# A four-layer cross-attention stack on one core: small layers' tails merged into single stages, one layer's keys computed in the tail before, and its first query group stored alone

## The chip, the core and the metric

The kernel runs on one core of a Trainium2 chip. It is one program, launched once, in 32-bit floats. The metric is the device time of one execution in microseconds (us). The core has five engines with an instruction stream each: TensorE (PE in the rows; PEld is its weight load), VectorE (DVE), ScalarE (ACT), GpSimd (POOL) and SyncE (SP), which here only issues transfers.

## What is computed

Four layers follow one another on 1024 tokens (4 batches of 256) with 256 features; the context has the same size. Layer 0 is a large attention block with 16 heads of 128 and is not touched. Layers 1 and 3 are alike (16 heads of 16, keys from the context and from the tokens), layer 2 has 32 query heads of 8 over 8 key heads. Cut to what matters:

```python
def layer_1_and_3(x, latents):                    # latents: the tokens, x: the context
    h = concatenate([x, latents], axis=1)
    q = latents @ q_w + q_b
    kmat, v = split(h @ kv_w + kv_b)
    attn_out = softmax(mask(q kmat / 16)) v
    attn_out = attn_out @ out_w + out_b + latents
    out = attn_out * rsqrt(mean(attn_out**2) + 1e-6) * postnorm_w
    return gelu(out @ mlp_w1 + mlp_b1) @ mlp_w2 + mlp_b2 + latents

def layer_2(hidden, context):
    q, k, v = hidden @ Wq + bq, context @ Wk + bk, context @ Wv + bv
    x = softmax(q k / sqrt(8) + mask) v @ Wo + bo + hidden
    return (x - mean) * rsqrt(var + 1e-6) * gamma + beta
```

The keys of layer 2 come from the context alone, so they don't depend on layer 1.

## The kernel before

The program is a row of stages. Each is a block in which every engine runs its own list of instructions, ordered by hand and tied by semaphores; at the end of a block all engines meet, so the next block starts when the last of them, SyncE with its waits on transfers included, is through. Activations lie in SBUF as 8 tiles of 128 tokens by 256 features (`core.x`, in the rows `x_tok`), and transposed as 2 chunks of 128 features (`kt`) by 1024 tokens, worked in halves of 512. Products that feed a softmax or an MLP are made from a high and a low part of each operand (`hi` is a rounded copy, `lo` the rest), which costs a copy on ScalarE and a subtraction on VectorE or GpSimd per tile.

Layers 1 and 3 run the stages `pair_projections` (p), `pair_attention` (s), `project_out` (o), `rms_turn` (r) and `mlp` (m). Layer 2 runs `turn` (t, it transposes the tokens), `wide_projections` (p), `wide_attention` (s), `project_out` (o) and `final_norm` (n). The prefix of a tile's name in the rows is the stage's letter.

- `project_out`: SyncE loads the output weight and the bias row; TensorE transposes the attention's output `o_all` (16 transposes into `t_ps`), VectorE copies the four chunks to `oT`, adds the bias row to the residual tile by tile, and then adds each product `y_ps` to it.
- `rms_turn`: SyncE loads the first MLP weight (`w1_raw`), ScalarE rounds it, GpSimd subtracts (`w1_lo`). VectorE takes the statistics of 8 tiles, GpSimd the power -0.5 of each half, ScalarE scales tiles 0 to 3, VectorE tiles 4 to 7, TensorE transposes, ScalarE and VectorE write the two parts of the MLP's input, `h_hi` and `h_lo`.
- `wide_projections`: TensorE makes keys (two groups of 512 tokens), then queries (four groups), then values. Each group goes VectorE (bias) to ScalarE (high) to VectorE (low) to SyncE, which stores it in HBM (`k_stack`, `q_stack`) and loads it again in the layout of the attention (`k_st`, `q_st`; `load_keys` and `load_queries` are four transfers each). The block ends when both query chunks are stored and the first half of batch 0's queries has come back.
- `wide_attention` goes over 32 quads of heads, eight for each batch; SyncE loads the queries and keys of the later ones beside it.
- `final_norm` takes the statistics, normalises, scales and shifts 8 tiles in a row on VectorE.

## Time and profile before

| | us |
|---|---|
| median of 3 executions | 1364.05 (1360.95 to 1368.05) |
| the profiled execution | 1362.59 |
| its span in the profile | 1360.8 |
| layer 1: last attention output to the MLP's first matmul | 873.53 to 899.38 |
| layer 2: last tile of layer 1 to the attention's first matmul | 947.69 to 979.64 |
| layer 2: last attention output to layer 3's first transpose | 1105.16 to 1132.71 |
| layer 3: last attention output to the MLP's first matmul | 1286.67 to 1312.69 |

The profile is of one execution. A row of the timeline gives the start, the time from start to end in us, engine, line, operation, tiles, and a count; in brackets how long the engine had stood idle and what released it (PEq and POOLq are the sequencers of those engines, and a line of `with nc.Block()` there is the meeting at a block's end). Instructions of one engine overlap a little, so a row of eight is shorter than eight single ones. An fp32 matmul stands as two records.

### The profile page before, as it was taken

How to read it: one execution, taken by the hardware profiler on the slowest of the kernel's cores; microseconds unless marked ns; L12 is line 12 of the kernel's file. 1: busy time of each engine (PE TensorE's matmuls, PEld its weight loads, DVE VectorE, ACT ScalarE, POOL GpSimd, SP SyncE). 2: the span in 40 equal slices, each digit the busy share in tenths (PEclk: the TensorE clock that was granted, in tenths of full speed). 3: DMA queues.
4: the chain of work that ended last, by engine and by line, in shares of the span. 5: the costliest groups of instructions: out<-in, count | busy, mean ns of one | idle time of the engine just before them, and what ended most of it. 6: DMA issues, size and time to landing. Idle time of an engine off the chain costs nothing. (4 is left out here: it accounts for less than half of the span.)

```text
span 1360.8 us, 27452 instructions
## 1 busy us (share of the span) xinstructions
PE 1222.3 (90%) x9144; PEld 1008.0 (74%) x9144; DVE 984.0 (72%) x2228; ACT 724.9 (53%) x1644; POOL 491.9 (36%) x638
## 2 busy tenths in 40 slices
PE   5999999999799999998699699869599977699969
PEld 5999999998699999997598355558377756455558
DVE  5778888778788788887564588474488865689464
ACT  5666566566666567666532277341166632177441
POOL 4744554453654454442240000030199940000030
PEclk9999999999899999999799599879799997699889
DMA  5111001100311110100305873020760013874020
GB/s 177 47 32 33 22 17 31 31 24 0 106 32 32 32 31 23 31 15 0 98 1 107 106 83 40 13 79 2 210 124 2 2 52 74 126 80 57 13 66 32
DMA packets 55406, 70.90 MB, mean 52 GB/s; under 512 B 6696, under 2 KB 47404, under 8 KB 52976
## 3 DMA queue, kind: packets, MB, share of 16 engines
q1 hardware_dynamic: 53704, 65.83, 23.3%
q10 hardware_dynamic: 1600, 3.76, 1.0%
q8 instruction: 57, 0.93, 0.3%
q14 instruction: 45, 0.37, 0.1%
HBM read 46.79 MB, written 8.13 MB: 40 GB/s over the span
## 5 line engine op out<-in xcount | busy, mean ns | idle before, releaser
L993 ACT ACTIVATE a_prob<-a_s_ps,a_negmax 128x257 f32<-128x257 f32 x256 | 119.0, 476 | 93.6 <-DVE a_negmax L1075 93.6
L2085 DVE TENSOR_REDUCE s_mx<-s_s_ps 128x2 f32<-128x1024 f32 x128 | 151.9, 1211 | 18.3 <-PE s_s_ps L2130 18.0
L2070 ACT ACTIVATE s_probT<-s_st_ps 128x512 f32<-128x512 f32 x256 | 132.2, 606 | 56.3 <-PE s_st_ps L2144 54.0
L934 POOL TENSOR_TENSOR x_v_hi<-a_v_sum,x_one 128x512 fp32r<-128x512 f32 x60 | 63.2, 1053 | 244.5 <-DVE a_v_sum L1064 244.4
L1874 POOL TENSOR_SCALAR s_below<-s_masked,s_mx 128x256 f32<-128x256 f32 x256 | 117.8, 480 | 28.8 <-DVE s_mx L1902 28.0
L605 POOL TENSOR_TENSOR rstd<-base,power 128x4 f32<-128x4 f32 x4 | 4.0, 1009 | 334.4 <-DVE base L622 334.4
L1090 DVE TENSOR_TENSOR a_pT_lo<-a_t_ps,a_pT_hi 128x512 fp32r<-128x512 f32 x128 | 88.2, 689 | 37.3 <-ACT a_pT_hi L1006 35.6
L1075 DVE TENSOR_REDUCE a_negmax<-a_s_ps 128x2 f32<-128x514 f32 x128 | 87.0, 688 | 23.8 <-PE a_s_ps L1136 23.7
L1902 DVE CUSTOM_DVE_ANT_0 s_masked<-s_s_ps,l_mask 128x256 f32<-128x256 f32 x256 | 90.7, 421 | 15.7 <-PE s_s_ps L1939 15.7
L1006 ACT ACTIVATE a_pT_hi<-a_t_ps 128x512 fp32r<-128x512 f32 x128 | 76.6, 599 | 46.8 <-PE a_t_ps L1190 43.2
L1134 PE MATMUL a_s_ps<-x_k_hi,x_q_hi 128*128 128x258 f32 x256 | 74.7, 292 | 11.2 <-ACT a_prob L993 5.4
L1887 ACT ACTIVATE s_probT<-s_st_ps 128x512 f32<-128x512 f32 x128 | 69.7, 595 | 28.2 <-PE s_st_ps L1949 28.1
L1134 PE MATMUL a_o_ps<-a_pT_hi,x_v_hi 128*128 128x256 f32 x256 | 81.1, 317 | 0.0
L2130 PE MATMUL s_s_ps<-l_k_st,l_q_st 49*128 49x512 f32 x192 | 67.5, 544 | 15.0 <-PEq L1583 8.6
L1009 ACT ACTIVATE a_oT_hi<-a_o_ps,a_hc 128x256 fp32r<-128x256 f32 x128 | 60.7, 474 | 37.0 <-PE a_o_ps L1136 29.7
L1190 PE MATMUL a_t_ps<-ident,a_prob 128*128 128x128 f32 x512 | 77.2, 273 | 3.3 <-ACT a_prob L1001 2.0
L936 POOL TENSOR_TENSOR x_v_lo<-a_v_sum,x_v_hi 128x512 fp32r<-128x512 f32 x60 | 77.4, 1290 | 4.7
L2144 PE MATMUL s_st_ps<-l_q_st,l_k_st 50*128 50x256 f32 x384 | 69.9, 337 | 10.0 <-DMA l_q_st<-s_mxT 9.8
L1136 PE MATMUL a_s_ps<-x_k_hi,x_q_lo 128*128 128x258 f32 x256 | 72.8, 285 | 0.0
L2144 PEld LDWEIGHTS s_st_ps<-l_q_st,l_k_st 50*128 50x128 f32 x384 | 47.9, 203 | 33.6 <-DMA l_q_st<-s_mxT 11.9
L1135 PE MATMUL a_s_ps<-x_k_lo,x_q_hi 128*128 128x258 f32 x256 | 72.7, 284 | 0.0
L1136 PE MATMUL a_g_ps<-a_wo_hi,a_oT_lo 128*128 128x256 f32 x256 | 72.6, 283 | 0.0
(293 smaller groups left out, 4047.2 us busy)
## 6 DMA issues: line engine op xcount, KB each, us to landing
a_wo_raw<-L_xattn_wo SPq DMA_DIRECT2D x16, 256.0 KB, 3.4
x_wqk_raw<-L_xattn_wq SPq DMA_DIRECT2D x31, 128.0 KB, 2.3
x_wqk_raw<-L_xattn_wk SPq DMA_DIRECT2D x31, 128.0 KB, 2.3
x_wv_raw<-L_xattn_wv SPq DMA_DIRECT2D x15, 256.0 KB, 3.2
l_k_st<-k_second SPq DMA_DIRECT2D x12, 256.0 KB, 9.3
l_k_st<-k_stack SPq DMA_DIRECT2D x16, 192.0 KB
l_q_st<-q_stack SPq DMA_DIRECT2D x12, 192.0 KB
x_vbias<-L_xattn_bias_v SPq DMA_DIRECT2D x2, 1024.0 KB, 7.1
```

The lines of the kernel that those rows point to most:

```text
L936: nc.gpsimd.tensor_tensor(lo, raw, hi.bitcast(F32), ALU.subtract).then_inc(z.v_split, 1)
L993: nc.scalar.activation(prob[:, n % 2, qt, 0:NK], s_ps[:, n % 2, qt, 0:NK], ACT.Exp, bias=negmax[:, n % 2, qt:qt + 1], accum_out=den[:, n % ...
L1075: nc.vector.tensor_reduce(negmax[:, n % 2], s_ps[:, n % 2, :, 0:NK], AX.X, ALU.max, negate=True).then_inc(z.max_done, 1)
L1090: nc.vector.tensor_tensor(pT_lo[:, n % 2], t_ps[:], pT_hi[:, n % 2].bitcast(F32), ALU.subtract).then_inc(z.t_out, 1)
L1134: nc.tensor.matmul(out, a_hi, b_hi, start=start, stop=False)
L1136: return nc.tensor.matmul(out, a_lo, b_hi, start=False, stop=stop)
L1190: mm = nc.tensor.transpose(t_ps[:, at:at + P], prob[:, n % 2, qt, kt * P:(kt + 1) * P], core.ident[:])
L1874: nc.gpsimd.tensor_scalar(below[:, i % 2, h, qt], masked[:, i % 2, h, qt], -1.0, mx[:, i % 2, h, qt:qt + 1], ALU.mult, ALU.add).then_inc(z ...
L1902: nc.vector.tensor_tensor_reduce(out=masked[:, i % 2, h, qt], in0=s_ps[:, h, qt], in1=mask[:, i // NQ * QT + qt], scale=1.0, scalar=-3.0e3 ...
L2070: nc.scalar.activation(probT[:, third % 2, n // 4, n // 2 % 2, n % 2], st_ps[:, u % 3], ACT.Exp, scale=c.scale).then_inc(z.exp_done, 1)
L2085: nc.vector.tensor_reduce(mx[:, i % 2, qt, a::2], s_ps[:, n % 2], AX.X, ALU.max).then_inc(z.max_done, 1)
L2144: mm = nc.tensor.matmul(st_ps[:, u % 3, j * S:(j + 1) * S], k[:, a, kt * P:(kt + 1) * P], q[:, a], start=True, stop=True)
```

## The change

Nothing is computed otherwise; the numbers are the same operations in other places.

- The stages `project_out` and `rms_turn` of layers 1 and 3 become one block, `project_and_rms`; `project_out` and `final_norm` of layer 2 become `project_and_scale`. In them VectorE and ScalarE copy two chunks each, VectorE takes a tile's statistics right behind its addition, and all scaling by the norm is ScalarE's (eight tiles instead of four).
- The output weight and bias row are loaded during the attention (`OutWeights`), and the bias is added to the residual there, by GpSimd: in layers 1 and 3 in `pair_attention`, into the memory of the late heads' high keys (`k_high`), in layer 2 in `wide_projections`, into `core.x`.
- The projection weights of layers 2 and 3 are loaded at the end of the attention before.
- The keys of layer 2 are made and stored in layer 1's tail (`WideKeys`); layer 1's `mlp` lets ScalarE wait for their three stores before its first instruction.
- `turn` is part of `wide_projections`, whose query groups now go by token half first. Only group 0 is stored there, by three transfers of 256 KB, and only batch 0's mask is loaded; groups 1 to 3 and the other masks are SyncE's in the attention.
- The MLP's `hid` buffer lies in `o_all`.

```diff
+    def keys(self, pe, half):
+        KW, core = self.front.KW, self.core
+        for kt in range(KT):
+            mm = self.nc.tensor.matmul(self.ps(half), core.wkv[:, kt, 0:KW], core.cT[:, kt, self.cols(half)],
+                                       start=(kt == 0), stop=(kt == KT - 1))
+        mm.then_inc(self.k_done, 1)
+
+    def high(self, act, half):
+        cols = self.cols(half)
+        act.wait_ge(self.k_done, half + 1)
+        self.nc.scalar.activation(self.f[:, cols], self.ps(half), ACT.Identity, bias=self.bias).then_inc(self.f_done, 1)
+        act.wait_ge(self.f_done, half + 1)
+        self.nc.scalar.activation(self.hi[:, cols], self.f[:, cols], ACT.Copy).then_inc(self.hi_done, 1)
+
+    def low(self, pool, half):
+        cols = self.cols(half)
+        pool.wait_ge(self.hi_done, half + 1)
+        self.nc.gpsimd.tensor_tensor(self.lo[:, cols], self.f[:, cols], self.hi[:, cols].bitcast(F32), ALU.subtract
+                                     ).then_inc(self.lo_done, 1)
+
+    def store(self, sp):
+
+        for part, (kept, slots) in enumerate(((self.hi, (0, 2)), (self.lo, (1,)))):
+            sp.wait_ge((self.hi_done, self.lo_done)[part], 2)
+            for n in slots:
+                sp.dma_start(self.front.k_stack[:, n], kept[:].bitcast(F32)).then_inc(self.front.k_stored, 16)
...
+                if wide:
+                    act.wait_ge(wide.k_stored, 3 * 16)
...
-            rms_turn(core, f"r{layer}", src, w, EPS, scale)
+            c, o_all, weights, dst = front
+            project_and_rms(core, f"r{layer}", c, o_all, weights, dst, w, EPS, scale, wide)
...
-                sp.dma_start(mask[:], ins["mask_Bx1xSxS2_ff0"].rearrange("b o (t p) k -> p (b o t) k", p=P)
-                             ).then_inc(mask_in, 16)
-
-                def stores(g):
-                    is_k, m, _ = groups[g]
-                    for part in range(2):
-                        sp.wait_ge((qk_hi, qk_lo)[part], g + 1)
-                        store(sp, part, is_k, m)
-
-                stores(1)
-                stores(3)
-                sp.wait_ge(k_stored, 16 * 3)
-                load_keys(c, sp, k_stack, k_st, 0, first_in)
-                stores(5)
-                sp.wait_ge(q_stored[0], 16 * 3)
-                load_queries(c, sp, q_stack, q_st, 0, slice(0, c.NQ // 2), first_in)
-                sp.wait_ge(mask_in, 16)
-                sp.wait_ge(q_stored[1], 16 * 3)
-                sp.wait_ge(first_in, 16 * 8)
+                pool.wait_ge(z.tile_turned, 2 * KT)
+                weights.add_row(pool, core.x, z.row_in)
...
+                sp.wait_ge(front.k_stored, 3 * 16)
+                load_keys(c, sp, front.k_stack, k_st, 0, z.first_in)
+                load_mask(core, sp, mask, 0, z.mask_in)
+                weights.load_row(sp, z.row_in)
+                for part in range(2):
+                    sp.wait_ge((z.q_hi, z.q_lo)[part], 1)
+                    q_late.store(front, sp, 0, (high(0), low(0)), part, z.q_stored)
+                sp.wait_ge(z.q_stored, 3 * 16)
+                load_queries(c, sp, front.q_stack, q_st, 0, slice(0, c.NQ // 2), z.first_in)
+                sp.wait_ge(z.mask_in, 16)
+                sp.wait_ge(z.first_in, 16 * 8)
...
+                    dve.wait_ge(z.q_done, g + 1)
+                    nc.vector.tensor_scalar(whole(g), q_ps[:, g], bq[:, m:m + 1], c.scale, ALU.add, ALU.mult
+                                            ).then_inc(z.q_f, 1)
+                    dve.wait_ge(z.q_hi, g + 1)
+                    nc.vector.tensor_tensor(low(g), whole(g), high(g).bitcast(F32), ALU.subtract).then_inc(z.q_lo, 1)
...
-                load_queries(c, sp, q_stack, q_st, 0, slice(NQ // 2, NQ), batch_in[0])
-                for b in range(1, B):
-                    load_keys(c, sp, k_stack, k_st, b, batch_in[b])
-                    load_queries(c, sp, q_stack, q_st, b, slice(0, NQ), batch_in[b])
+                def store(g):
+                    for part in range(2):
+                        q_late.store(front, sp, g, (q_late.hi[:, g - 1], q_late.lo[:, g - 1]), part, q_stored[g - 1])
+
+                store(1)
+                load_mask(core, sp, mask, 1, batch_in[1])
+                sp.wait_ge(q_stored[0], 3 * 16)
+                load_queries(c, sp, front.q_stack, q_st, 0, slice(NQ // 2, NQ), batch_in[0])
+                load_keys(c, sp, front.k_stack, k_st, 1, batch_in[1])
+                load_queries(c, sp, front.q_stack, q_st, 1, slice(0, NQ), batch_in[1])
+                for g in (2, 3):
+                    store(g)
+                for b in range(2, B):
+                    load_mask(core, sp, mask, b, batch_in[b])
+                    load_keys(c, sp, front.k_stack, k_st, b, batch_in[b])
+                for g in (2, 3):
+                    sp.wait_ge(q_stored[g - 1], 3 * 16)
+                for b in range(2, B):
+                    load_queries(c, sp, front.q_stack, q_st, b, slice(0, NQ), batch_in[b])
+                weights.load(sp, z.out_in)
+                sp.wait_ge(z.out_in, 16 + core.load_projections(sp, 3, z.out_in))
...
+                pool.wait_ge(unit_in[1], c.UNIT + 4 * 16)
+                pool.wait_ge(unit_in[2], c.UNIT)
+                weights.add_row(pool, a_tok, z.row_loaded)
...
+                    if first == 11:
+                        weights.load_row(sp, z.row_loaded)
+                        weights.load(sp, z.out_in)
+                sp.wait_ge(z.out_in, 16 + (core.load_projections(sp, 2, z.out_in) if L == 1 else 0))
...
+    def add_row(self, pool, dst, row_in):
+
+        pool.wait_ge(row_in, 16)
+        for t in range(TT):
+            self.core.nc.gpsimd.tensor_tensor(dst[:, t], self.core.x[:, t], self.row[:], ALU.add)
...
+    def copy_vector(self, dve, half):
+        out, ps = self.place(0, half)
+        dve.wait_ge(self.z.turned, KT * half + 1)
+        self.nc.vector.tensor_copy(out, ps).then_inc(self.z.copied_dve, 1)
+
+    def copy_scalar(self, act, half):
+        out, ps = self.place(1, half)
+        act.wait_ge(self.z.turned, KT * half + 2)
+        self.nc.scalar.activation(out, ps, ACT.Copy).then_inc(self.z.copied_act, 1)
+
+    def product(self, pe, t):
+        if t % 4 == 0:
+            pe.wait_ge(self.z.copied_dve, t // 4 + 1)
+            pe.wait_ge(self.z.copied_act, t // 4 + 1)
+        wait(pe, self.z.y_out, t - 3)
+        for kt in range(KT):
+            mm = self.nc.tensor.matmul(self.y_ps[:, t % 4, 0:D], self.oT[:, kt, t * P:(t + 1) * P],
+                                       self.weights.w[:, kt], start=(kt == 0), stop=(kt == KT - 1))
+        mm.then_inc(self.z.y_done, 1)
+
+    def add(self, dve, t):
+        dve.wait_ge(self.z.y_done, t + 1)
+        self.nc.vector.tensor_tensor(self.dst[:, t], self.y_ps[:, t % 4, 0:D], self.dst[:, t], ALU.add
+                                     ).then_inc(self.z.y_out, 1)
+
+    def observe(self, dve, t):
+        dve.wait_ge(self.z.y_out, t + 1)
+        observe(self.core, dve, self.dst, t, self.z)
...
+                low(0)
+                deviation(core, pool, 0, z, 0)
+                low(1)
+                deviation(core, pool, 1, z, 1)
+                if keys:
+                    for half in range(2):
+                        keys.low(pool, half)
...
+                out.turn(pe)
+                for t in range(TT):
+                    out.product(pe, t)
+                for half in range(2):
+                    if keys:
+                        pe.wait_ge(z.y_out, half + 5)
+                        keys.keys(pe, half)
+                    pe.wait_ge(z.normed_act, HT * (half + 1))
+                    for kt in range(KT):
+                        for i in range(HT):
+                            mm = nc.tensor.transpose(turned[:, KT * half + kt, i * P:(i + 1) * P],
+                                                     normed[:, HT * half + i, kt * P:(kt + 1) * P], core.ident[:])
+                        mm.then_inc(z.tile_turned, 1)
...
+                    out.copy_scalar(act, half)
+                ahead.prepare_scalar(act, z)
+                for t in range(4):
+                    normalise(t)
+                if keys:
+                    keys.high(act, 0)
+                for n in range(2):
+                    high(n)
+                for t in range(4, TT):
+                    normalise(t)
+                if keys:
+                    keys.high(act, 1)
+                for n in range(2, 4):
+                    high(n)
...
```

What VectorE does in layer 1's tail, where `o` and `r` name the stages, `a_o_all` and `a_k_high` the sum of residual and projection. Before:

```order
L2241 COPY o_oT<-o_t_ps 128x512 x4
L2245 TENSOR_TENSOR a_o_all<-x_tok,o_b_row 128x256 x8
L2249 TENSOR_TENSOR a_o_all<-o_y_ps,a_o_all 128x256 x8
L2197 UNCONDITIONAL_BRANCH
L609 UNCONDITIONAL_BRANCH
L614 BN_STATS stats<-a_o_all 128x6 x4
L617 BN_AGGR mv<-stats 128x2 x4
L620 TENSOR_TENSOR r_msq<-mv 128x4
```

Now (the first half; the second is alike, without the copies):

```order
L2212 COPY r_oT<-r_t_ps 128x512 x2
L2231 TENSOR_TENSOR a_k_high<-r_y_ps,a_k_high 128x256
L164 BN_STATS stats<-a_k_high 128x6
L2231 TENSOR_TENSOR a_k_high<-r_y_ps,a_k_high 128x256
L164 BN_STATS stats<-a_k_high 128x6
L2231 TENSOR_TENSOR a_k_high<-r_y_ps,a_k_high 128x256
L164 BN_STATS stats<-a_k_high 128x6
L2231 TENSOR_TENSOR a_k_high<-r_y_ps,a_k_high 128x256
L164 BN_STATS stats<-a_k_high 128x6
L2242 BN_AGGR mv<-stats 128x2 x4
L2332 TENSOR_TENSOR r_msq<-mv 128x4
L2334 SCALAR_TENSOR_TENSOR base<-r_msq,mv 128x4
```

The eight additions of the bias are gone, two of the four copies too, and every second row is a statistic where all of them stood behind the last addition.

ScalarE in the same tail, `w_w_hi` being the rounded first MLP weight and `r_k_f`, `r_k_hi` layer 2's keys. Before:

```order
L2204 UNCONDITIONAL_BRANCH
L588 UNCONDITIONAL_BRANCH
L1352 ACTIVATE w_w_hi<-w_w_raw 128x1024 x2
L593 ACTIVATE r_normed<-a_o_all,rstd 128x256 x4
L597 ACTIVATE w_h_hi<-r_turned,cols 128x512 x4
L583 UNCONDITIONAL_BRANCH
```

Now:

```order
L2298 UNCONDITIONAL_BRANCH
L2217 ACTIVATE r_oT<-r_t_ps 128x512 x2
L1299 ACTIVATE w_w_hi<-w_w_raw 128x1024 x2
L2308 ACTIVATE r_normed<-a_k_high,rstd 128x256 x4
L574 ACTIVATE r_k_f<-r_y_ps,cols 64x512
L576 ACTIVATE r_k_hi<-r_k_f 64x512
L2303 ACTIVATE w_h_hi<-r_t_ps,cols 128x512 x2
L2308 ACTIVATE r_normed<-a_k_high,rstd 128x256 x4
L574 ACTIVATE r_k_f<-r_y_ps,cols 64x512
L576 ACTIVATE r_k_hi<-r_k_f 64x512
L2303 ACTIVATE w_h_hi<-r_t_ps,cols 128x512 x2
L2259 UNCONDITIONAL_BRANCH
```

The two copies, four more scalings and the four instructions on the keys have come in, the scalings in two groups of four, each ahead of the two chunks of `w_h_hi` that need it.

SyncE in layer 2's projections. Before:

```order
L1751 DMA l_mask<-mask_Bx1xSxS_ff 128x8x256
L1735 DMA k_stack<-p_k_hi 8x8x1024 x2
L1735 DMA k_stack<-p_k_lo 8x8x1024
L1739 DMA q_stack<-p_q_hi 16x8x1024 x2
L1739 DMA q_stack<-p_q_lo 16x8x1024
L1692 DMA l_k_st<-k_stack 24x8x256 x4
L1739 DMA q_stack<-p_q_hi 16x8x1024 x2
L1739 DMA q_stack<-p_q_lo 16x8x1024
L1699 DMA l_q_st<-q_stack 24x4x256 x4
L1741 UNCONDITIONAL_BRANCH
```

Now:

```order
L1644 DMA l_k_st<-k_stack 24x8x256 x4
L1650 DMA l_mask<-mask_Bx1xSxS_ff 128x2x256
L2175 DMA a_b_out<-L_xattn_bo 128x256
L1672 DMA q_stack<-p_q_hi 16x8x512 x2
L1672 DMA q_stack<-p_q_lo 16x8x512
L1656 DMA l_q_st<-q_stack 24x4x256 x4
L1703 UNCONDITIONAL_BRANCH
```

The stores of the keys have gone into layer 1's tail, and one query store of half the size stands ahead of the four loads, where two full ones stood.

## Rows read from the trace of the kernel before

**Rows 1.** Busy time by engine (with counts), TensorE's granted clock, DMA share and GB/s.

```profile
885.00:899.30 14.30, 3.93 (x16) 3.13 (x16) 12.07 (x28) 6.46 (x10) 6.70 (x4) 0.61 0.22 73
```

**Rows 2.** Timeline of VectorE from the end of layer 1's attention to its MLP.

```profile
873.24 0.29 DVE L2096 TENSOR_TENSOR a_o_all<-s_ox_ps,s_rden 128x128 f32<-128x128 f32 x1
874.51 2.48 DVE L2241 COPY o_oT<-o_t_ps 128x512 f32<-128x512 f32 x4 [0.99 <-PE o_t_ps L2222]
...
885.02 1.41 DVE L614 BATCH_NORM_STATS2 stats<-a_o_all 128x6 f32<-128x256 f32 x4 [0.32 <-PEq L2197]
...
890.22 5.32 DVE L626 TENSOR_SCALAR r_normed<-a_o_all,rstd 128x256 f32<-128x256 f32 x4 [1.12 <-POOL rstd L605]
...
897.47 1.60 DVE L630 SCALAR_TENSOR_TENSOR w_h_lo<-r_turned,cols,w_h_hi 128x512 fp32r<-128x512 f32 x2 [0.61 <-ACT w_h_hi L597]
```

**Rows 3.** Timelines of SyncE's queue, ScalarE, GpSimd and TensorE in the same stretch.

```profile
884.97 0.89 SPq L1347 DMA_DIRECT2D w_w_raw<-L_xattn_mlp_w  x2
...
888.71 1.06 ACT L1352 ACTIVATE w_w_hi<-w_w_raw 128x1024 fp32r<-128x1024 f32 x1 [16.24 <-DMA w_w_raw<-L_xattn_mlp_w]
...
890.15 4.71 POOL L1357 TENSOR_TENSOR w_w_lo<-w_w_raw,w_w_hi 128x1024 fp32r<-128x1024 f32 x2
...
880.55 3.69 PE L2232 MATMUL o_y_ps<-o_w,o_oT 128*128 128x256 f32 x16 [0.15 <-DVE a_o_all L2249]
892.75 1.97 PE L640 MATMUL r_turned<-ident,r_normed 128*128 128x128 f32 x8 [8.50 <-ACT r_normed L593]
...
899.38 0.76 PE L1411 MATMUL m_h_ps<-w_h_hi,w_w_hi 128*128 128x512 f32 x1 [1.81 <-PEq L583]
```

**Rows 4.** Timeline of TensorE at the start of layer 3's MLP.

```profile
1312.69 0.47 PE L1411 MATMUL m_h_ps<-w_h_hi,w_w_hi 128*128 128x512 f32 x1 [1.81 <-PEq L583]
```

**Rows 5.** Timelines of VectorE, ScalarE, TensorE and SyncE's queue in layer 2's projections.

```profile
947.27 0.42 DVE L1474 TENSOR_TENSOR x_tok<-m_y_ps,x_tok 128x256 f32<-128x256 f32 x1 [2.45 <-PE m_y_ps L1413]
...
960.48 0.75 DVE L1799 TENSOR_SCALAR p_q_f<-p_qk_ps,cols 128x512 f32<-128x512 f32 x1 [0.37 <-PE p_qk_ps L1779]
961.14 0.68 DVE L1803 TENSOR_TENSOR p_q_lo<-p_q_f,p_q_hi 128x512 fp32r<-128x512 f32 x1
...
961.26 0.63 ACT L1822 ACTIVATE p_q_hi<-p_q_f 128x512 fp32r<-128x512 f32 x1 [1.09 <-DVE p_q_f L1799]
...
955.02 7.13 PE L1779 MATMUL p_qk_ps<-x_xT,wq 128*128 128x512 f32 x16
...
979.64 0.81 PE L1939 MATMUL s_s_ps<-l_k_st,l_q_st 24*128 24x256 f32 x8 [13.12 <-PEq L1741]
...
960.20 1.80 SPq L1739 DMA_DIRECT2D q_stack<-p_q_hi  x2
...
968.69 2.03 SPq L1739 DMA_DIRECT2D q_stack<-p_q_lo  x1
970.77 10.37 SPq L1699 DMA_DIRECT2D l_q_st<-q_stack  x8
```

**Rows 6.** Transfers of line 1739, the stores of `q_stack`: six of 512 KB.

```profile
DMA to landing us min/median/max: 4.9/6.9/8.9
```

**Rows 7.** Timelines of VectorE, GpSimd and TensorE in layer 2's tail.

```profile
1104.93 0.23 DVE L1914 TENSOR_TENSOR a_o_all<-s_ox_ps,s_rden 128x64 f32<-128x64 f32 x1
...
1114.02 0.43 DVE L2249 TENSOR_TENSOR x_tok<-o_y_ps,x_tok 128x256 f32<-128x256 f32 x1 [0.67 <-PE o_y_ps L2232]
...
1129.65 2.76 DVE L2296 TENSOR_TENSOR x_tok<-x_tok,n_b_row 128x256 f32<-128x256 f32 x8
...
1114.85 2.55 POOL L100 TENSOR_TENSOR parts_w_parts<-wkv,parts_w_parts 128x512 fp32r<-128x512 f32 x2
...
1109.44 8.86 PE L2232 MATMUL o_y_ps<-o_w,o_oT 128*128 128x256 f32 x32 [2.03 <-DMA o_w<-L_xattn_Wo]
...
1132.71 3.65 PE L1625 MATMUL p_turned<-ident,x_tok 128*128 128x128 f32 x16 [14.41 <-PEq L2262]
```

**Rows 8.** Timeline of VectorE in layer 1's MLP, while GpSimd subtracts there.

```profile
909.64 1.78 DVE L1457 TENSOR_TENSOR m_hid_lo<-m_hid,m_hid_hi 128x512 fp32r<-128x512 f32 x1
```

536 lines of the change are left out of this document (265 added, 271 removed).

## The prediction

> **What bounds the kernel now.** I first read the busy table by engine: TensorE is busy 90% of the span, so what can be won quickly lies where it stands. The 40 slices put these places between layers, and the timelines of the engines show four of them. In layer 1's tail the attention's last output ends at 873.53 [rows 2] and the MLP's first matmul starts at 899.38 [rows 3]: 25.85 us. In them VectorE works nearly without a gap, first on copies and sums, then on statistics [rows 2], and TensorE waits 8.5 us for the scaled tiles [rows 3]. The chain there is transposes, copies, products, sums, statistics, power, scaling, transposes, `h_hi`, `h_lo`, with a meeting of all engines in the middle, and the MLP weight is asked for only behind that meeting, at 884.97 [rows 3]. Layer 3's tail is the same, 1286.67 to 1312.69, 26.02 us [rows 4]. Layer 2's tail, 1105.16 to 1132.71, is 27.55 us, and TensorE stands 14.41 us in it, while VectorE passes over all tiles one pass after the other [rows 7]. The fourth place is layer 2's start, 947.69 to 979.64, 31.95 us: VectorE and ScalarE are through long before, and TensorE waits 13.12 us for the block's end [rows 5], which is SyncE's wait for stores of 512 KB that take 4.9 to 8.9 us to land [rows 6]. The last of them was issued at 970.72, and 8 us behind that is the block's end.
>
> **The change, part by part.** Times are counted from the end of the last attention output (0).
>
> Layer 1's tail. Transposes run 0.3 to 2.3 as now. The first copy starts about 1.0 in [rows 2] and takes some 0.7; with ScalarE taking every second one, none holds back the products, which before began at 3.1 and waited for the output weight and for VectorE. A weight that is loaded in the attention costs SyncE's queue one issue there and no one waits for it. Four tiles of product take 3.69 [rows 3], with the overlap some 0.87 each, so eight end at 9.3. VectorE adds (0.42, [rows 7]) and takes the statistic (1.41 for four, 0.41 singly, [rows 2]) in about 0.81 per tile: it keeps up with TensorE in the first half. The moments and the two small operations cost 0.8 per half, so the second half ends at 10.75 and its `base` at 11.55. The power takes 1.0 on GpSimd. The weight is asked for at 0.3; from issue to ScalarE's start it was 3.74 [rows 3], so ScalarE rounds it from 4.1 to 6.4 (1.06 each and a gap), GpSimd subtracts the first half from 5.2 to 7.6 (4.71 for two, [rows 3]), makes the first power until 8.65, subtracts again until 11.1, and makes the second power by 12.6. ScalarE scales four tiles by 10.4 (0.42 each). TensorE has meanwhile made the keys' first half: the queries' four groups take 7.13, so one group 1.8 [rows 5]: 9.3 to 11.1. Then come one after the other on ScalarE: two key operations (0.7 and 0.63) until 12.5, two `h_hi` until 13.8, four scalings until 15.45, two key operations until 16.8, two `h_hi` until 18.05. VectorE's last `h_lo` ends at 18.85, the last key store is issued at about 19.0, and with 0.3 for the meeting the MLP starts at **19.3**: 6.5 less. The four key instructions cost 2.6 of ScalarE's time here; without them it would be 17 to 18. The MLP's new wait for the key stores stands before ScalarE's table load. By the shortest landing of the larger stores, 4.9 [rows 6], the last one lands at 24, some 4.7 into the MLP, and by half that (half the bytes) at 21.5. Behind that wait stand the table load and the first activations, and TensorE can go on for four groups of 1.4 to 1.7 before it misses them. I take 0 for it, 3 at the other end.
>
> Layer 3's tail has no keys in it: the same chain gives 17.8 with all at full speed. The weight landed a microsecond later there, and its transposes may run at half clock, so I take **18.5**: 7.5 less.
>
> Layer 2's tail. Product and sums as above, 10.8. GpSimd now has to subtract the next layer's three weights (2.55 for two, [rows 7]) before it can make the first power: ScalarE rounds them from 3.1 on, GpSimd is through at 7.6, and the power, asked for at 7.3, is there at 8.6, when VectorE has just done tile 5. That costs nothing. ScalarE scales the tiles; VectorE is left with 16 operations of 0.345 (2.76 for eight, [rows 7]), in pairs with a wait of its own result between, 1.45 per two tiles: 11.4 to 17.45. The end is at **17.75**: 9.8 less. GpSimd's subtractions in this stretch left VectorE's addition at 0.43 [rows 7].
>
> Layer 2's start, counted from 947.69. The meeting between `turn` and the projections goes (3.4 us with the first copies), and the keys with their 3.6 on TensorE. Transposes end at 2.3, query group 0 at 4.1, its bias, high and low parts (0.75, 0.63, 0.68, [rows 5]) at 6.4. SyncE has issued the key loads, mask and row by 5.0; two stores took it 1.80 [rows 5], half rows less, so the last store is issued at about 7.5. These three are 256 KB each instead of six of 512 KB. From both sides: at the shortest landing, 4.9 [rows 6], they are in HBM at 12.4; with half of that at 10. I take 11.5. Four loads at some 0.6 are issued by 14, and landing takes 3.4 (the 3.74 of the MLP weight, [rows 3], less ScalarE's start): **17.4**, 14.5 less. Between 15.5 and 21. VectorE's work is no later than that: four groups in series at 2.3 are through at 13.3, the values at 15.7.
>
> Beside them run GpSimd's eight new additions, from about 8 on, 5 us by the 2.55 for two of twice the size [rows 7]. A VectorE subtraction of SBUF operands beside a GpSimd one in the MLP took 1.78 [rows 8] where it takes 0.68 alone [rows 5]. Three of the `q_lo` can be hit: up to 3.3 more, VectorE through at 19.0 instead of 15.7. The Trainium skill, SBUF — State Buffer, in the summary of its contention rules, says that a VectorE instruction with two SBUF inputs and a GpSimd instruction that reads SBUF exclude one another for their whole length. By that rule the block would end at up to 19.0 and not at 17.4, the sum 1.6 worse; the row agrees with the rule. I keep 17.4, since only what exceeds the transfers counts, and 19.0 goes into the range.
>
> The clock. TensorE's granted clock is 0.61 of full speed over layer 1's tail [rows 1]: it stood, and it starts the MLP at half speed (1.2 GHz), 0.76 for its first matmul [rows 3], while layer 3's MLP starts at full speed, 0.47 [rows 4], because 16 transposes ran just before it in one piece. Layer 1's MLP took 48.3, layer 3's 45.5 from first matmul to last sum: 2.8 for the clock. In the new tails the transposes stand in two pieces of 1 us with gaps of 2 to 4 us about them, so I expect layer 3's MLP to begin slowly too: **+2.8**; layer 1's has the keys in between, I take no change there.
>
> In the pair attentions GpSimd is idle, and its eight additions and SyncE's two loads cost nothing: VectorE's work there reads PSUM. The second half of batch 0's queries must be there four quads after the start of `wide_attention`, 14 us; SyncE stores, waits and loads them by 12 (2 for the stores, 4 to land, 2.4 and 3.4 for the loads). The price of a delay is small: 0 to 4.
>
> Sum: 6.5 + 7.5 + 9.8 + 14.5 - 2.8 = 35.5. The profiled execution took 1362.59 for a span of 1360.8, so 1327.1 for it; its time lies 1.46 below the median of 1364.05, so the median goes to **1328.5**.
>
> **The rivals.** (a) The waits take half the room: landing at the long end (+3.5 at layer 2's start), the second query half late (+4), the MLP's wait for the key stores (+3): about +10, 1338. For it speaks that store landings vary between 4.9 and 8.9 [rows 6]; against it that less is in flight. (b) The clock stays up through both tails: neither MLP starts slowly, 2.8 + 2.8 better, and ScalarE's order fits better than I think: 1321. (c) The change doesn't shorten the blocks: each tail is held by a chain I think covered, in layers 1 and 3 GpSimd with weight and power in one list, at layer 2's start the stores. Then only the copies' 1.4 and a meeting of 0.6 are won in each tail: 1358. Against it: GpSimd's list is 7.8 long and starts at 5. (d) Slower: `wide_attention` is starved. Its loads for batches 2 and 3 stand in SyncE's queue behind six more stores and a wait for them. From the point at which a round of stores and loads takes longer than the 30 us of eight quads, every batch adds the rest. It would have to take 42 us each time, three times 12, to eat 36 of gain: 1366 and more. A round is reckoned at 20.
>
> **How the numbers follow.** The forecast has a chance of 0.62, (a) 0.2, (b) 0.13, (c) 0.03, (d) 0.02. The range reaches from 1319 (b, with the short landings) to 1341 (a, with the contention's 1.6 and slow transposes). A measurement of this kernel can tell about 0.5% (7 us) from no change. The chance of slower is that of (d), that of no difference most of (c).
>
> **What would show it.** In the profile after: the MLPs start 19 and 18.5 us behind the last attention output, layer 3's transposes 17.8 behind layer 2's; the attention of layer 2 starts 17.4 us behind the last sum of layer 1, with TensorE waiting some 2 us at that meeting; `q_lo` rows of over 1 us show the contention; a wait of TensorE for `l_q_st` in quad 4 shows (a); the first matmul of an MLP at 0.47 or 0.76 shows the clock. I would be wrong above all if a store of 256 KB lands no faster than one of 512 KB.

## The result, and the profile after

| | before | changed |
|---|---|---|
| median of the runs, us | 1363.16 (1360.95 to 1368.05) | 1325.91 (1323.9 to 1328.42) |
| ratio to before | 1 | 0.9723, 95% interval 0.9691 to 0.9755 |
| profiled execution; its span | 1362.59; 1360.8 | 1325.39; 1323.2 |
| mean granted clock | 0.939 | 0.950 |

The change takes 37.3 us off the median (forecast 1328.5). The stages can be measured between rows that both kernels have: the end of the last attention output (`a_o_all`), the first matmul into `m_h_ps`, the end of the MLP's last sum (`x_tok<-m_y_ps`), the first `s_s_ps` matmul, and the first `p_turned` transpose. "Layer 3 up to the tail" holds its projections and its attention.

| stage, us | before | changed | gain |
|---|---|---|---|
| up to the end of layer 1's attention | 873.53 | 873.48 | 0.1 |
| layer 1's tail | 25.85 | 19.98 | 5.9 |
| MLP 1 | 48.31 | 47.71 | 0.6 |
| layer 2's start | 31.95 | 16.21 | 15.7 |
| layer 2's attention | 125.52 | 126.26 | -0.7 |
| layer 2's tail | 27.55 | 16.74 | 10.8 |
| layer 3 up to the tail | 153.96 | 155.02 | -1.1 |
| layer 3's tail | 26.02 | 18.15 | 7.9 |
| MLP 3 | 45.54 | 47.14 | -1.6 |

The gains add up to 37.6, the difference of the spans is 37.6. The three tails and layer 2's start give 40.3; the other stages together take 2.7 more than before.

Layer 1's tail, from the timelines of VectorE, TensorE, ScalarE and SyncE's queue of the changed kernel (start, length, engine and line, operation, count, in brackets the wait before it and what ended it). It answers [rows 2, 3]:

```profile
873.19 0.29 DVE L2074 TENSOR_TENSOR a_o_all<-s_ox_ps,s_rden 128x128 f32<-128x128 f32 x1
875.64 7.14 PE L2225 MATMUL r_y_ps<-a_w_out,r_oT 128*128 128x256 f32 x32
882.50 1.71 ACT L2308 ACTIVATE r_normed<-a_k_high,rstd 128x256 f32<-128x256 f32 x4 [2.46 <-POOL rstd L181]
885.04 0.16 DVE L2334 SCALAR_TENSOR_TENSOR base<-r_msq,mv 128x4 f32<-128x4 f32 x1
...
889.92 1.24 ACT L2303 ACTIVATE w_h_hi<-r_t_ps,cols 128x512 fp32r<-128x512 f32 x2
891.39 1.28 SPq L589 DMA_DIRECT2D k_stack<-r_k_lo  x1
893.46 0.76 PE L1358 MATMUL m_h_ps<-w_h_hi,w_w_hi 128*128 128x512 f32 x1 [3.53 <-PEq L2259]
```

The products start 2.2 behind the last output (3.1 before), the eight run through in 7.14, ScalarE scales the first four tiles while VectorE still sums the last four, and the chain ends with the last `h_hi` at 891.16 and the last key store at 892.67.

Layer 2's start, from the timelines of all engines; it answers [rows 5]:

```profile
940.75 0.42 DVE L1423 TENSOR_TENSOR x_tok<-m_y_ps,x_tok 128x256 f32<-128x256 f32 x1 [2.45 <-PE m_y_ps L1360]
947.95 0.60 SPq L1672 DMA_DIRECT2D q_stack<-p_q_lo  x1
950.58 6.40 POOL L2182 TENSOR_TENSOR x_tok<-x_tok,a_b_out 128x256 f32<-128x256 f32 x8 [6.05 <-DMA a_b_out<-L_xattn_bo]
950.82 1.04 DVE L1759 TENSOR_TENSOR l_q_lo<-p_q_f,l_q_hi 128x512 fp32r<-128x512 f32 x1 [0.70 <-ACT l_q_hi L1776]
952.33 1.57 SPq L1656 DMA_DIRECT2D l_q_st<-q_stack  x4
953.21 1.14 DVE L1759 TENSOR_TENSOR l_q_lo<-p_q_f,l_q_hi 128x512 fp32r<-128x512 f32 x1 [0.70 <-ACT l_q_hi L1776]
956.83 0.22 DVE L1764 TENSOR_TENSOR l_v_st<-p_v_ps,bv_row 128x64 f32<-128x64 f32 x1 [0.48 <-PE p_v_ps L1745]
957.38 0.81 PE L1910 MATMUL s_s_ps<-l_k_st,l_q_st 24*128 24x256 f32 x8 [0.58 <-PEq L1703]
```

SyncE issues the last of the three stores 7.4 us behind the last sum, has them 3.8 later and issues the loads. Before, TensorE waited 13.12 at this meeting [rows 5]; now 0.58. Three things end here close together: the last of the query and key loads lands at 956.49 (the trace's semaphore events), GpSimd's additions end at 956.98, VectorE's last value tile at 957.05. So in this execution it is VectorE that ends last, 0.33 before the first scores.

The ends of the two other tails, from the timelines of VectorE, TensorE and SyncE's queue; they answer [rows 4, 7]:

```profile
1094.55 0.76 DVE L2416 TENSOR_TENSOR x_tok<-x_tok,o_g_row 128x256 f32<-128x256 f32 x2
...
1099.33 0.75 DVE L2419 TENSOR_TENSOR x_tok<-x_tok,o_b_row 128x256 f32<-128x256 f32 x2
1100.38 3.65 PE L1577 MATMUL p_turned<-ident,x_tok 128*128 128x128 f32 x16 [7.43 <-PEq L2366]
...
1269.94 1.80 PE L2294 MATMUL r_t_ps<-ident,r_normed 128*128 128x128 f32 x8 [2.73 <-ACT r_normed L2308]
1273.55 0.77 PE L1358 MATMUL m_h_ps<-w_h_hi,w_w_hi 128*128 128x512 f32 x1 [1.81 <-PEq L2259]
```

The clock shows in the last three: sixteen transposes take 3.65, as they did before [rows 7], where the same sixteen take 1.94 at layer 2's start; eight take 1.80 here and 1.09 in the tail's first half; and MLP 3 starts with 0.77 where it had 0.47 [rows 4]. The granted clock over the end of that tail, from the view by stretches (length, busy time of PE, PEld, DVE, ACT, POOL, granted clock, DMA share, GB/s):

```profile
1265.00:1268.00 3.00, 1.09 (x8) 0.86 (x8) 2.38 (x11) 2.25 (x5) 2.53 (x2) 1.00 0.00 0
1268.00:1271.00 3.00, 1.06 (x6) 1.06 (x7) 0.94 (x2) 1.86 (x6) 0.14 (x1) 0.86 0.00 0
1271.00:1274.00 3.00, 1.19 (x5) 0.81 (x4) 1.50 (x2) 1.78 (x3) 0.00 (x0) 0.50 0.00 0
```

### The profile page after: what moved, and what is told of

Same layout as the page of the kernel before. It is cut to its first block and busy times, and to the rows that moved or that the text cites. A ratio compares the mean times of both kernels' runs of the same rounds, so it can differ in the third digit from the quotient of the medians.

```text
span 1323.2 us, 27397 instructions
## 1 busy us (share of the span) xinstructions
PE 1218.8 (92%) x9144; PEld 1005.9 (76%) x9144; DVE 961.0 (73%) x2179; ACT 737.7 (56%) x1670; POOL 511.6 (39%) x664
## 5 line engine op out<-in xcount | busy, mean ns | idle before, releaser
L2063 DVE TENSOR_REDUCE s_mx<-s_s_ps 128x2 f32<-128x1024 f32 x128 | 151.9, 1211 | 18.0 <-PE s_s_ps L2108 17.7
L1037 DVE TENSOR_TENSOR a_pT_lo<-a_t_ps,a_pT_hi 128x512 fp32r<-128x512 f32 x128 | 88.2, 689 | 37.3 <-ACT a_pT_hi L953 35.6
L2182 POOL TENSOR_TENSOR a_k_high<-x_tok,a_b_out 128x256 f32<-128x256 f32 x16 | 11.1, 733 | 223.7 <-DMA a_b_out<-L_xattn_out_b 223.7
L2122 PEld LDWEIGHTS s_st_ps<-l_q_st,l_k_st 50*128 50x128 f32 x384 | 48.4, 204 | 33.6 <-DMA l_q_st<-s_mxT 12.0
L1081 PE MATMUL a_g_ps<-a_wo_hi,a_oT_hi 128*128 128x256 f32 x256 | 72.5, 283 | 0.0
```

What stands on the lines that cost most here:

```text
L1037: nc.vector.tensor_tensor(pT_lo[:, n % 2], t_ps[:], pT_hi[:, n % 2].bitcast(F32), ALU.subtract).then_inc(z.t_out, 1)
L1081: nc.tensor.matmul(out, a_hi, b_hi, start=start, stop=False)
L2063: nc.vector.tensor_reduce(mx[:, i % 2, qt, a::2], s_ps[:, n % 2], AX.X, ALU.max).then_inc(z.max_done, 1)
L2122: mm = nc.tensor.matmul(st_ps[:, u % 3, j * S:(j + 1) * S], k[:, a, kt * P:(kt + 1) * P], q[:, a], start=True, stop=True)
```

## The experiments

Each is an edit of the changed kernel. The stages of all of them, in us between the rows named above, are of the execution that was profiled; the median is that of all executions, with that of the kernel before, run beside it. The edits were run in three groups on different chips, so medians of different groups are compared by their ratio to before:

| kernel | tail 1 | MLP 1 | start 2 | tail 2 | layer 3 | tail 3 | MLP 3 | median (of before beside it) |
|---|---|---|---|---|---|---|---|---|
| changed_again | 19.98 | 47.67 | 16.47 | 16.75 | 154.98 | 18.33 | 47.05 | 1326.44 (1364.68) |
| all_groups | 19.98 | 48.28 | 26.14 | 16.73 | 151.40 | 17.57 | 47.69 | 1331.56 (1362.02) |
| keys_back | 18.16 | 47.03 | 24.24 | 16.75 | 152.91 | 18.34 | 46.84 | 1331.18 (1362.02) |
| keys_back_no_row | 18.33 | 46.91 | 24.06 | 16.75 | 154.09 | 18.35 | 47.04 | 1328.40 (1364.68) |
| no_row | 19.98 | 47.76 | 16.12 | 16.73 | 154.76 | 18.67 | 48.37 | 1323.81 (1365.31) |
| residual_back | 26.32 | 48.08 | 15.22 | 22.66 | 155.19 | 23.43 | 47.76 | 1338.12 (1362.02) |
| adds_back | 20.55 | 47.70 | 15.90 | 21.58 | 151.18 | 19.86 | 48.30 | 1329.91 (1365.31) |
| sums_first | 23.96 | 47.35 | 16.48 | 19.59 | 151.27 | 22.76 | 46.91 | 1338.11 (1362.02) |
| keys_kept | 20.07 | 47.79 | 16.72 | 16.73 | 154.61 | 18.27 | 46.91 | 1324.90 (1365.31) |
| filled | 20.64 | 47.57 | 16.83 | 17.61 | 153.89 | 17.77 | 45.53 | 1323.81 (1365.31) |
| late_stores | 18.85 | 48.27 | 17.28 | 16.74 | 154.86 | 18.27 | 47.05 | 1324.52 (1364.68) |
| best | 18.86 | 45.53 | 16.49 | 16.74 | 151.22 | 17.76 | 45.50 | 1316.93 (1364.68) |

A stage that an edit doesn't touch repeats within 0.1 in tails 1 and 2, some 0.6 in layer 2's start, 1.1 in tail 3, 0.9 in MLP 1 and 1.5 in MLP 3. Layer 3's part scatters by 4. Most of the scatter of the MLPs and of layer 3 goes with the time at half clock, as is shown further on.

**The changed kernel again**, as the measure for keys_back_no_row, late_stores and best, which were run beside it.

> The changed kernel as it is, on the same chip and beside the same runs as the three others of this call, so that they can be compared with it directly. Expected by every theory: 0.972 of the kernel before, 1325 to 1327.

1326.44 (1324.62 to 1328.39), ratio 0.972, interval 0.9703 to 0.9737. The result stands.

**What the first group's own store is worth.** All four groups are stored in the block, and batch 0's queries are loaded behind all twelve stores:

```diff
-                for part in range(2):
-                    sp.wait_ge((z.q_hi, z.q_lo)[part], 1)
-                    q_late.store(front, sp, 0, (high(0), low(0)), part, z.q_stored)
-                sp.wait_ge(z.q_stored, 3 * 16)
-                load_queries(c, sp, front.q_stack, q_st, 0, slice(0, c.NQ // 2), z.first_in)
+                for g in range(len(groups)):
+                    for part in range(2):
+                        sp.wait_ge((z.q_hi, z.q_lo)[part], g + 1)
+                        q_late.store(front, sp, g, (high(g), low(g)), part, z.q_stored)
+                sp.wait_ge(z.q_stored, 12 * 16)
+                load_queries(c, sp, front.q_stack, q_st, 0, slice(0, c.NQ), z.first_in)
```

> The changed kernel with the separate first store undone: all four query groups (12 stores of 256 KB) are stored in the projections' block, and batch 0's queries are loaded there at once, behind a wait for all twelve. Everything else stays. In the changed kernel the last sum of layer 1's MLP ends at 941.17 and the first scores of layer 2 start at 957.38: 16.2 us. Theory (stores and the way back set this place): the last q_lo ends at about 954.4, the last store is issued at 955, lands 4 to 5 later, four loads of twice the size take 2 to issue and 4 to land: 965 to 967, so 24 to 26 us, 8 to 10 more than now, and the whole 1334 to 1336. Rival (the work of VectorE and GpSimd, which ended at 957.0 and 957.1, holds the block anyway, and transfers cost little): 2 to 3 more at most, 1328 to 1329.

The start takes 26.14 instead of 16.21, 9.9 more: the theory's size, not the rival's. The rows of SyncE's queue (timeline of all_groups):

```profile
947.68 0.59 SPq L1672 DMA_DIRECT2D q_stack<-p_q_lo  x1
...
953.89 0.53 SPq L1672 DMA_DIRECT2D q_stack<-l_q_lo  x1
959.38 1.62 SPq L1656 DMA_DIRECT2D l_q_st<-q_stack  x4
```

The last store is issued at 954.42, 6.1 later than in the changed kernel, and waited for until 959.38, 5.0 against the 3.8 of the three alone. The loads, twice as large here, take 2.6 more until the first scores, which start 6.0 behind the last issue. So storing and loading one group alone carries 9.9 of the 15.7 of this stage. The ratio to before is 0.9760 (0.9724 to 0.9796), only some 5 us worse than the changed kernel and not the 8 to 10 expected of the whole: layer 3's part was 3.6 shorter in this profile.

**Layer 2's keys where they were**, in layer 2's projections, behind query group 0; no keys in layer 1's tail, no wait in MLP 1:

```diff
                     mm.then_inc(z.q_done, 1)
+                    if g == 0:
+                        keys.keys(pe, 0)
...
+                        keys.keys(pe, 1)
...
```

> The changed kernel with layer 2's keys made in layer 2's projections again (behind query group 0), not in layer 1's tail; the MLP of layer 1 has then no wait for their stores. Theory: layer 1's tail becomes as long as layer 3's, 18.15 instead of 19.98 (1.8 less, the keys' four operations on ScalarE); layer 2's start gets the keys' two matmul groups before query groups 1 to 3 (3.6 us on TensorE), and the key loads wait for stores that are issued at some 951.5 by the old clock and land 3.8 later: the start grows from 16.2 to about 20, by 3.5 to 4. The whole becomes 2 worse: 1328. Rival (the keys lie in the shadow of the queries' way to HBM and back): the start grows by less than 1 and the whole becomes 1 to 1.5 better: 1324.5. Second rival (the wait for the key stores had cost the MLP of layer 1 something): MLP 1 falls from 47.7 by up to 3; theory says it stays at 47.7 within 0.3.

The tail is 1.8 shorter, as the theory had it. MLP 1 is 0.7 shorter, where the theory had no change within 0.3 (its cause is the clock, as is shown under "The clock"). The start grows by 8.0, not by 3.5 to 4, and the ratio to before is 0.9773 (0.9735 to 0.9811). Timelines of VectorE and GpSimd:

```profile
948.37 4.66 DVE L1768 TENSOR_TENSOR l_q_lo<-p_q_f,l_q_hi 128x512 fp32r<-128x512 f32 x1 [0.70 <-ACT l_q_hi L1785]
947.65 5.95 POOL L2194 TENSOR_TENSOR x_tok<-x_tok,a_b_out 128x256 f32<-128x256 f32 x8
```

A subtraction that takes 0.69 alone took 4.66 beside GpSimd's additions, which end at 953.60, 0.6 behind it. That looked like the missing 4, and I tested it.

**The same without GpSimd's additions.**

```diff
-                weights.add_row(pool, core.x, z.row_in)
+                pool.wait_ge(z.row_in, 16)
```

> The run with layer 2's keys back in layer 2's projections, without GpSimd's eight additions there (the output bias of layer 2 is left out of the sum). In the run with them one q_lo of VectorE took 4.66 beside GpSimd's additions, instead of 0.69, and layer 2's start took 24.2. Theory (GpSimd's additions hold a VectorE instruction with both inputs in SBUF): q_lo is 0.69 four times, and the start takes 20 to 20.5, 4 less; the keys' place is then worth 3.9 less 1.8 of the tail, about 2. Rival (something else held it, the stores or the semaphore): q_lo still over 4, start at 24.

Half a miss. The contention is shown: `q_lo` is 0.69 four times. But the start stays at 24.06, so the 4 us had cost at most 0.2; the loads ended as late without them. In keys_back the contention had used up VectorE's room: its last value tile ended at 961.25, 0.32 before the first scores. Timelines of VectorE, SyncE's queue and TensorE:

```profile
950.81 0.69 DVE L1768 TENSOR_TENSOR l_q_lo<-p_q_f,l_q_hi 128x512 fp32r<-128x512 f32 x1 [0.70 <-ACT l_q_hi L1785]
951.56 3.53 SPq L1656 DMA_DIRECT2D l_q_st<-q_stack  x4
956.18 1.60 SPq L1644 DMA_DIRECT2D l_k_st<-k_stack  x4
963.84 0.81 PE L1922 MATMUL s_s_ps<-l_k_st,l_q_st 24*128 24x256 f32 x8 [5.68 <-PEq L1704]
```

The query loads took 3.53 to issue behind the key stores instead of 1.57, the key loads could be issued only at 956.18, and the first scores start 6.1 behind the last of them. The keys' own way to HBM and back is what the move into layer 1's tail takes off this place: 7.8 there, for 1.7 in the tail.

**Does the contention cost the changed kernel anything?** The same edit in the changed kernel.

> The changed kernel without GpSimd's eight additions beside layer 2's projections; the output bias of layer 2 is left out of the sum. In the changed kernel GpSimd's additions, VectorE's list and the query loads all ended at 957.0 to 957.3, and the first scores start 16.2 after layer 1's last sum. Theory (transfers set the end): at most 0.5 better, since q_lo 2 and 3 fall from 1.04 and 1.14 to 0.69 off the path. Rival (contention and GpSimd's own end set it): 1.0 better, 15.2, as the run without both the row's load and its additions had it (15.22).

The start takes 16.12 instead of 16.21 and 16.47: 0.1 to 0.35 less, as the theory had it. But its reason, that transfers set the end, holds only with the additions gone. The ends in VectorE's and TensorE's timelines of no_row, and in GpSimd's and TensorE's of changed_again:

```profile
957.51 0.23 DVE L1763 TENSOR_TENSOR l_v_st<-p_v_ps,bv_row 128x64 f32<-128x64 f32 x1 [0.22 <-PE p_v_ps L1744]
959.02 0.81 PE L1909 MATMUL s_s_ps<-l_k_st,l_q_st 24*128 24x256 f32 x8 [1.55 <-PEq L1703]
...
952.12 6.49 POOL L2182 TENSOR_TENSOR x_tok<-x_tok,a_b_out 128x256 f32<-128x256 f32 x8 [6.29 <-DMA a_b_out<-L_xattn_bo]
958.95 0.81 PE L1910 MATMUL s_s_ps<-l_k_st,l_q_st 24*128 24x256 f32 x8 [1.46 <-PEq L1703]
```

In no_row VectorE is through 1.3 before the first scores, and the last load lands 0.51 before them (the trace's semaphore events). In changed_again the last load landed 1.1 before them and GpSimd's last addition ended 0.34 before; in the changed kernel's first profile it was VectorE's last tile. With the 0.51 behind the last load, the transfers alone would have let the scores start 0.4 to 0.6 earlier there. That is the most that additions and contention cost. The medians don't settle it: without the additions the ratio to before was 0.9687 (0.9672 to 0.9702) against 0.9720 (0.9703 to 0.9737), some 4.5 us better on another chip, but the one execution that was profiled was the slowest of its five, 1329.18, so no stage can be named for this gain.

**Weights, rows and additions back in the tails.** SyncE loads the bias row and the weight there first, VectorE makes eight additions before the sums.

```diff
                 for half in range(2):
                     out.copy_vector(dve, half)
+                out.add_row(dve)
...
```

> The changed kernel with the output weights, the bias row and the additions of residual and bias back in the three tails: SyncE loads row and weight there first, VectorE makes eight additions before the sums. Theory: the weight lands some 4.5 us after the last attention output, where the first product started at 2.2 (1257.57 against 1255.40 in layer 3), and VectorE's additions (8 by 0.35 = 2.8) end at about 7 where the first sum started at 3.3: each tail grows by 3.5 to 4, together 10.5 to 12: tails of 23.7, 20.5 and 22, the whole 1337. Rival (VectorE catches up, since it waits later in the tail for the scaled tiles): under 1.5 per tail, 1330.

The tails 1, 2 and 3 grow by 6.3, 5.9 and 5.3, where 3.5 to 4 were expected. What was missing is the clock in tails 1 and 3, and contention in tail 2. VectorE's and TensorE's timelines in layer 3's tail, whose last output ends at 1266.02, and VectorE's additions in layer 2's:

```profile
1269.81 2.77 DVE L2193 TENSOR_TENSOR a_k_high<-x_tok,a_b_out 128x256 f32<-128x256 f32 x8 [1.23 <-DMA a_b_out<-L_xattn_out_b]
1271.49 9.97 PE L2228 MATMUL r_y_ps<-a_w_out,r_oT 128*128 128x256 f32 x32 [3.21 <-DMA a_w_out<-L_xattn_out_w]
...
1091.93 5.83 DVE L2193 TENSOR_TENSOR x_tok<-x_tok,a_b_out 128x256 f32<-128x256 f32 x8 [1.21 <-DMA a_b_out<-L_xattn_bo]
```

TensorE stands 3.21 for the weight, and the products then take 9.97 instead of 7.14, at a granted clock of 0.71 over these 9.97: the sums come 1.71 apart instead of 0.87 at first. In tail 2 the eight additions take 5.83 instead of 2.77, beside GpSimd's subtractions of the next weights; the next run shows the same. (The row was loaded ahead of the weight here, and the kernel before did it the other way round, so this is more than the exact undoing; its products had started 3.1 behind the last output.)

**Only the additions back**, weights and rows early:

```diff
-                weights.add_row(pool, a_tok, z.row_loaded)
...
                 for half in range(2):
                     out.copy_vector(dve, half)
+                out.add_row(dve)
...
```

> The changed kernel with output weights and bias rows still loaded in the attentions, but the additions of residual and bias on VectorE in the three tails, before the sums. In the run with the loads in the tails as well, layer 3's tail was 23.43 instead of 18.15: TensorE waited 3.21 for the weight, and its products then stood 9.97 instead of 7.14. Theory: the larger part of that is the weight and the clock that falls while TensorE stands, so with the weight early VectorE's 8 by 0.35 = 2.8 remain: tails of 22.8, 19.5 and 21, the whole about 1334. TensorE starts its products at 2.2 behind the last output and stops after four tiles. Rival (the additions alone make the difference): tails of 25 to 26, 22 and 23, 1341.

Tail 1 grows by 0.6, tail 3 by 1.7, tail 2 by 4.8; the 2.8 for each that the theory had fits none of them, though the weight and the clock are the larger part in tails 1 and 3, as it said. In layers 1 and 3 VectorE catches up, since its list has gaps further on where it waits for ScalarE. In layer 2's tail it has none, and the additions meet GpSimd's subtractions of the next weights. Timelines of VectorE and TensorE:

```profile
1087.36 6.03 DVE L2196 TENSOR_TENSOR x_tok<-x_tok,a_b_out 128x256 f32<-128x256 f32 x8
1093.88 3.69 PE L2229 MATMUL o_y_ps<-a_w_out,o_oT 128*128 128x256 f32 x16 [3.12 <-DVE x_tok L2236]
```

Eight additions that take 2.77 alone take 6.03 there. So the addition in the attention is worth about 7 us over the three tails, and 3.3 of them are contention that the old order had not shown.

**The order within VectorE's list.** Sums first, then statistics, in all three tails, still in one block:

```diff
+                for t in range(TT):
+                    out.add(dve, t)
                 for half in range(2):
                     for t in range(half * HT, (half + 1) * HT):
-                        out.add(dve, t)
                         out.observe(dve, t)
...
```

> The changed kernel with one order changed: in all three tails VectorE makes the eight sums first and the statistics of the tiles after them, four and four, as before the change, but still in one block. Theory (it is the interleaving that starts the chain early): the sums end at 9.8 after the last output, base of the first half at about 12.2 where it was 7.8, that of the second at 14.6 where it was 11.6; the second half's chain is then 3 later, the first half's 4.4, and the tails grow by 3 to 4.5 each, 10 to 12 together: 1337. Rival (the gain came from what is in one block and from ScalarE's share, the order of VectorE's list matters little): under 1 each, 1328.

4.0, 2.9 and 4.6 more in tails 1, 2 and 3: the theory holds, the rival falls. The interleaving by tile is worth 11.4 of the 24.6 that the three tails have gained. (The profiled execution, 1331.70, was the fastest of five; the stages are compared within it.)

**The wait in MLP 1.** The rounded keys lie in a buffer that the MLP doesn't use, so that ScalarE has nothing to wait for:

```diff
-                if wide:
-                    act.wait_ge(wide.k_stored, 3 * 16)
```

> The changed kernel with the rounded keys of layer 2 in a buffer that the MLP doesn't use, so that ScalarE has no wait for their stores at the start of layer 1's MLP. Theory (four banks of PSUM cover it): the table load moves from 896.44 to about 893.5, the first gelu to about 895.5, and the MLP stays at 47.7 within 0.3, since TensorE is busy without a gap in both; the whole 1326. Rival (ScalarE's late start delays the high and low parts that the second product needs): MLP 1 becomes 1 to 3 shorter.

MLP 1 takes 47.79 against 47.71 and 47.67, with ScalarE's table load at 892.97, just before the MLP's first matmul, instead of 3 us into it. The wait costs nothing at the clock that this MLP had, as predicted.

**The clock in the tails.** TensorE turns the identity into free PSUM wherever it waits there:

```diff
+                    out.fill(pe, turned[:, KT * half, 0:P], (12, 18)[half])
                     pe.wait_ge(z.normed_act, HT * (half + 1))
...
```

> The changed kernel with transposes of the identity into free PSUM wherever TensorE waits in the three tails: 12 before the first turned half, 18 before the second, 12 at the end of tails 1 and 3, 16 and 6 for each scaled tile in tail 2. Theory (the clock falls because TensorE stands there): the granted clock stays at 1.0, the second eight transposes of layer 3's tail take 1.09 instead of 1.80, the MLPs' first matmul 0.47 instead of 0.77, layer 3's projections begin with 16 transposes in 1.9 instead of 3.65; layer 3's MLP takes 45.5 instead of 47.1, layer 1's 46, tails 1 and 3 become 0 to 0.7 shorter: 5 to 6 together, 1320 to 1321. Rival (the fillers hold up the real transposes, which stand behind them in TensorE's list, or the clock doesn't count such work): no gain, or up to 2 worse, 1326 to 1328.

The clock does what the theory says. View by stretches, the end of layer 3's tail, and TensorE's timeline:

```profile
1268.00:1272.00 4.00, 3.24 (x30) 3.00 (x29) 1.59 (x3) 3.16 (x7) 0.55 (x1) 1.00 0.00 0
1272.00:1276.00 4.00, 3.27 (x18) 2.63 (x17) 1.31 (x3) 2.27 (x3) 0.00 (x0) 1.00 0.31 70
...
1273.47 0.47 PE L1358 MATMUL m_h_ps<-w_h_hi,w_w_hi 128*128 128x512 f32 x1 [0.73 <-PEq L2263]
```

MLP 3 takes 45.53, what it took before the change, so the 1.6 are the clock. MLP 1 starts with 0.47 as well and still takes 47.57. That was not expected, and ScalarE's timeline tells why:

```profile
893.96 0.71 SPq L1342 DMA_DIRECT2D m_w_raw<-L_xattn_mlp_w  x1
902.70 0.63 ACT L1398 ACTIVATE m_w_hi<-m_w_raw 128x512 fp32r<-128x512 f32 x1 [2.87 <-DMA m_w_raw<-L_xattn_mlp_w]
```

The second weight comes 8.7 us behind its issue, and ScalarE stands 2.87 for it; MLP 3 has it 5.7 behind. Ahead of it in SyncE's queue are the three key stores. Besides, the fillers made tail 1 0.7 and tail 2 0.9 longer; that real transposes stood behind them is the likely reason, not tested by itself. The ratio to before, 0.9686 (0.9669 to 0.9702) against 0.9720, is a gain of some 4.6 where 5 to 6 were expected.

**The key stores behind the second weight.** With the keys in the spare buffer, their stores can be issued in the MLP's block:

```diff
                 sp.dma_start(b2_row[:], ins[b2].rearrange("(o n) -> o n", o=1).broadcast_to([P, D])).then_inc(b2_in, 16)
+                if wide:
+                    for part, n in ((wide.hi, 0), (wide.hi, 2), (wide.lo, 1)):
+                        sp.dma_start(wide.k_stack[:, n], part.bitcast(F32)).then_inc(wide.k_stored, 16)
...
```

> The changed kernel with layer 2's rounded keys in a buffer that the MLP doesn't use, and their three stores issued in the MLP's block, behind the load of its second weight, instead of ahead of it in the tail. In the changed kernel the load of 1 MB is issued at 893.40, 0.7 behind the last key store, and ScalarE gets it at 902.14, 8.7 later, where layer 3's MLP had it 5.6 later in the kernel before (1312.64 to 1318.29); ScalarE's waiting there holds up TensorE. Theory (the stores ahead of it make the load late): the second weight is there 5 to 6 after its issue; MLP 1 takes 46.9 to 47.1, what layer 3's takes with the same slow start, instead of 47.7; the tail ends 0.5 earlier, since no store is issued behind VectorE's last h_lo; together 1.1 to 1.3 better. Rival (the load is late for another reason): still 8 to 9, MLP 1 at 47.7.

The tail is 1.1 shorter, twice the estimate. The weight lands 6.2 behind its issue, as the theory had it (semaphore events), but MLP 1 takes 48.27 and not 47. The clock stayed at half speed for longer behind the start, 5.8 us and not 4.6, and all_groups, with 5.9 us of it and the late weight, took 48.28: while the clock is down, the early weight gains nothing. The ratio to before, 0.9697 (0.9676 to 0.9719), is not clearly apart from the changed kernel's. Stretches of late_stores, whose MLP 1 starts at 895.23:

```profile
895.00:898.00 3.00, 2.77 (x7) 2.22 (x8) 0.00 (x0) 1.28 (x1) 0.00 (x0) 0.50 0.50 113
898.00:901.00 3.00, 3.00 (x9) 2.32 (x8) 0.43 (x1) 0.96 (x2) 0.00 (x0) 0.50 0.91 310
901.00:904.00 3.00, 3.00 (x15) 2.47 (x14) 1.95 (x4) 1.90 (x4) 0.36 (x1) 0.99 0.52 207
```

And of the changed kernel, where it starts at 893.46:

```profile
893.40:896.00 2.60, 2.54 (x6) 2.09 (x7) 0.00 (x0) 0.00 (x0) 0.00 (x0) 0.50 0.62 227
896.00:899.00 3.00, 3.00 (x10) 2.33 (x10) 0.43 (x1) 2.33 (x3) 0.00 (x0) 0.65 0.76 257
```

**All that helped, together**, and one thing more: in the last two rounds of the pair attentions, where no scores are left, a product of 128 by 512 stands in the place of each score step.

```diff
+                        elif kind == "S" and third is not None:
+                            repeat(n)
...
```

> Three things together: the late key stores of the run above; the filling transposes in the three tails, fewer than before (none before the first turned half of tail 1, 8 before the second, 20 there in tail 3, and none for the last two tiles of tail 2, since the fillers had held the meetings up by 0.7 to 0.9); and one product of 128 by 512 in place of each missing score step in the last two rounds of both pair attentions, where the granted clock fell to 0.72 and the last three rounds took 17.7 (137.0 to 154.7 from the layer's start) and in other runs 14.4. Theory: the clock stays at 1.0 through the last rounds, and these take 14.5 to 15 in layer 3 (2.5 to 3 less) and as much less in layer 1; MLP 1 takes 45.5 to 46 as its second weight comes early and its clock is full; MLP 3 45.5; layer 3's projections begin at full speed; the tails stay at 19.4, 16.8 and 17.8. In all 11 to 13 less than the changed kernel: 1313 to 1315. Rival (the fillers in the last rounds stand before shifted scores that ScalarE waits for, and cost what the clock gives): 1319 to 1320, with rounds of 5.9.

1316.93 (1313.82 to 1320.89), ratio to before 0.9657, interval 0.9637 to 0.9677; the changed kernel beside it had 0.9703 to 0.9737. So it beats both kernels, by 9.5 us against the changed one, where 11 to 13 were expected. MLP 1 takes 45.53, the same as MLP 3: with the stores out of the way the second weight was used 6.0 behind its issue. (ScalarE's wait for the key stores is gone here too; its row in filled names the weight, for which it stood 2.87 after that wait was over.) From the timelines of SyncE's queue and ScalarE:

```profile
889.67 0.37 SPq L1343 DMA_DIRECT2D m_w_raw<-L_xattn_mlp_w  x1
895.67 0.63 ACT L1400 ACTIVATE m_w_hi<-m_w_raw 128x512 fp32r<-128x512 f32 x1 [0.86 <-DMA m_w_raw<-L_xattn_mlp_w]
```

Neither edit had done it alone: with the clock up, the weight was late; with the weight early, the clock was down. Layer 3's first scores come 34.0 behind the start of its projections instead of 37.3. What missed is the filling of the last rounds. The last three took 17.0 in both layers, against 17.7 in layer 1 and 17.8 in layer 3 of the changed kernel; the clock still fell for one stretch in each, where it had fallen for two. The gain there was 0.7, where 2.5 to 3 were forecast.

## Why the prediction was right

**Where it waits, and on what.** The four places and their order of size held. The gain of the profiled execution is 2.1 more than forecast: the four places gave 2.0 more, the clock cost 1.2 less in MLP 3, MLP 1 gave 0.6 that wasn't forecast, and two stages taken at 0 cost 1.8. That the 1.8 lay on the other side, and so kept the total near the forecast, is luck. Taken by its terms:

| term | predicted | measured |
|---|---|---|
| layer 1's tail | 19.3 | 19.98 |
| layer 3's tail | 18.5 | 18.15 |
| layer 2's tail | 17.75 | 16.74 |
| layer 2's start | 17.4 | 16.21 |
| MLP 3, clock | +2.8 | +1.6 |
| MLP 1 | 0 | -0.6 |
| second half of the queries, attention 2 | 0 | +0.7 |
| layer 3's projections and attention | 0 | +1.1 |

**Layer 1's tail.** The chain came as it was worked out: second `base` 11.7 behind the last output (11.55 predicted), last `h_hi` 17.7 (18.05), last `h_lo` 18.5 (18.85), last key store 19.2 (19.0). The miss of 0.7 is the meeting: I put it at 0.3, and the MLP started 0.8 behind the last store. In layer 3's tail, where VectorE's `h_lo` ends last, it was 0.3 (1271.64 + 1.61 to 1273.55). Without the stores in it the tail is 1.1 shorter (late_stores). The keys' price of 2.6 was sized as ScalarE's time in one row; keys_back shows 1.8.

**Layer 2's tail.** VectorE began the affine operations at 10.9, 0.5 earlier than reckoned, and the eight pairs took 5.53 where I had 6.05: the wait for its own result was smaller than I took it for.

**Layer 2's start.** The last store was issued at 7.4 (7.5), the stores were waited for until 11.2 (11.5, from both sides 10 to 12.4). The term that was too large is the issue of the loads: 0.6 each by the old row, 0.39 in the new. The last load had landed at 15.3, and the transfers alone would have allowed 15.8. What ended at 15.9 was VectorE's list, forecast at 15.7 without contention, and at 15.8 GpSimd's additions, forecast at 13: they began at 9.4 instead of 8 and took 6.4 instead of 5. So the number fits, but the term that ends last was another, by 0.4. The sentence on which I would have been wrong, that a store of 256 KB lands no faster than one of 512, didn't come true: from issue to landing the three took 3.9, 4.0 and 4.4, against 4.9 to 8.9 [rows 6]. Size alone doesn't make it so: six such stores that SyncE issued in the attention, at 966.91 and later, right behind twelve loads, took 9.9 to 11.1. all_groups shows what storing one group alone is worth.

**Contention.** I let it cost nothing and kept 1.6 in the range. It happened, at the small end (1.04 and 1.14 instead of 0.69), and together with GpSimd's own end it cost at most 0.4 to 0.6. That holds for this alignment only. keys_back shows the same pair of instructions at 4.66. The rule quoted from the Trainium skill, SBUF — State Buffer, in its summary of contention, speaks of one instruction against one; GpSimd's additions are 0.74 each, so 4.66 covers five of them, and VectorE did not get its turn in between. The row decides: the price to put into a range is up to the length of the whole run of GpSimd instructions, 6 us here, not that of one.

**The clock.** That MLP 3 would start slowly was right, and filled shows the cause. The size is the term that was wrong: 2.8, the difference of the two MLPs before the change, measured 1.6. A slow start has no fixed price, since it depends on how long the half clock lasts behind it. Stretches of MLP 1 in the kernel before, from 899.38 on:

```profile
902.00:905.00 3.00, 3.00 (x8) 2.30 (x7) 0.43 (x1) 0.82 (x2) 0.00 (x0) 0.50 1.03 353
905.00:908.00 3.00, 3.00 (x14) 2.43 (x13) 1.76 (x4) 1.84 (x4) 0.18 (x1) 0.95 0.36 91
```

And of MLP 3 in the changed kernel, from 1273.55 on:

```profile
1276.00:1279.00 3.00, 3.00 (x13) 2.40 (x12) 0.52 (x2) 1.38 (x2) 0.00 (x0) 0.84 0.90 308
```

The first stood at half clock for 5.9 us behind its first matmul and took 48.31, the second for 3.4 and took 47.14. The fourteen profiles (before, the changed kernel twice, eleven edits) have two such MLPs each. With the time at half clock behind the first matmul (from the clock records that the granted clock of a stretch is the mean of), and the time from the second weight's issue to ScalarE's first use of it:

| MLP | at half clock | weight used after | took |
|---|---|---|---|
| MLP 3, before | 0 | 5.7 | 45.54 |
| MLP 1, best | 0 | 6.0 | 45.53 |
| MLP 1, filled | 0 | 8.7 | 47.57 |
| MLP 1, keys_back | 3.2 | 6.7 | 47.03 |
| MLP 3, changed | 3.4 | 6.7 | 47.14 |
| MLP 1, changed | 4.6 | 8.7 | 47.71 |
| MLP 1, all_groups | 5.9 | 8.7 | 48.28 |
| MLP 1, late_stores | 5.8 | 7.8 | 48.27 |
| MLP 1, before | 5.9 | 7.8 | 48.31 |
| MLP 3, no_row | 6.1 | 7.9 | 48.37 |

Of the 28 MLPs, 26 took 45.5 and 0.47 for each us at half clock, within 0.04. So the price is about half of the time at half clock, and the step that was mis-sized is that time: 2.8 is the price of the 5.9 us that MLP 1 had before, MLP 3 now had 3.4. That MLP 1 would stay as it was (0 predicted, 0.6 less measured) missed only the same thing: its half clock was 4.6 us instead of 5.9, and 0.47 times the difference is 0.6. What decides how long it lasts isn't shown.

The two exceptions have little or no half clock and the late weight: MLP 1 of filled, which is 2.05 over, and that of sums_first (3.4 us at half clock, weight used after 8.5), which is 0.24 over. That fits a second brake, the late weight, that shows only when the clock is up: in the changed kernel it costs nothing that this sum leaves room for, with the clock up it costs 2 (in filled ScalarE's wait for the stores is still in too, and was not tested by itself at full clock). The prediction asked who waits for the stores (ScalarE, at no cost, as keys_kept shows), not what is queued behind them. In the nine profiles with the three key stores ahead of it the weight of MLP 1 was used 8.2 to 8.9 behind its issue, in the five without them it landed after 6.0 to 6.6. By the Trainium skill, DMA: Bandwidth & Descriptors, in the section on queues, rings and completion order, each DMA engine takes the descriptors of a queue in order, and a completion is reported only behind all earlier writes of that engine. The rows agree: 8.7 behind the three stores in filled, 6.0 without them in best.

**What is open.** Layer 3's part took 1.1 more and layer 2's attention 0.7 more than before, with little changed in the first beside GpSimd's additions and the loads of the output weight and row. Layer 3's part takes 151.2 to 155.2 in the edits that don't touch it, and the longer ones stand longer at half clock: 33.6 to 33.7 us in the three of 151.2 to 151.4, 38.8 before, 40.1 in the changed kernel. So the 1.1 goes with 1.3 us more at half clock; why the clock fell for longer isn't shown. The forecast of no cost for the queries' second half holds in that TensorE never waited for `l_q_st` at quad 4. Layer 2's attention took 125.3 to 128.1 in the edits, so its 0.7 is within what it scatters by.

**The rivals.** (a) did not come: the first stores landed at the short end, and neither wait cost anything. Of (b) the clock did not come, the shorter chains in tails 2 and 3 did. (c) and (d) are out: copies and meeting alone cannot give 24.6 in the tails, of which sums_first takes 11.4 away and adds_back 7.1, and layer 2's attention was not starved.

## What to carry to other kernels

Of a step that is moved ahead, look at what stands behind its DMAs in the same queue, not only at who waits for them: three stores of 256 KB made a weight load 2.7 us later (filled against best). Two brakes can hide each other, since what they cost doesn't add up; when a theory's edit brings nothing, look for the second one before giving up the first. And where TensorE stands in a tail, look at its granted clock at the end of it: the price is paid in the stage behind, 1.3 to 2.9 here, half of the time that it stays at half clock. Where several lists end within half a microsecond, as at layer 2's start, look at the row before the meeting in more than one profile before naming what set the end.

## What the runs showed of the hardware

TensorE's granted clock fell in the last rounds of the pair attentions in most of the profiled runs, though the profile shows it busy nearly throughout. Stretches of the changed kernel at the end of layer 3's attention:

```profile
1237.00:1243.00 6.00, 6.00 (x48) 3.05 (x48) 1.02 (x4) 3.44 (x8) 0.00 (x0) 0.72 0.01 3
1243.00:1249.00 6.00, 6.00 (x46) 3.15 (x48) 0.50 (x2) 4.21 (x9) 0.00 (x0) 0.77 0.00 0
```

And of all_groups at the same place:

```profile
1247.00:1252.00 5.00, 4.93 (x51) 2.74 (x51) 0.88 (x5) 3.99 (x10) 0.00 (x0) 1.00 0.01 4
1252.00:1257.00 5.00, 4.93 (x49) 2.86 (x50) 0.49 (x2) 3.98 (x10) 0.00 (x0) 1.00 0.00 0
```

The last three rounds of layer 3 took 17.8 in the first and 14.5 in the second, with the same instructions. Of the thirteen profiles without fillers there three had the short form (all_groups, adds_back, sums_first). Part of the scatter in the column of layer 3 is this. What decides between the two isn't shown; a product in the place of each missing score step (best) moved it by 0.7.

A VectorE instruction of four columns (`r_msq`) took 1.81 in sums_first instead of 0.16, and 0.61 in layer 1's tail of the changed kernel, each time beside a GpSimd subtraction of 2.35 or 2.36. The instruction's own length says nothing of what such contention costs it.
